# Two layers in one launch on one Trainium2 core: the second layer re-staged into three overlapping stages, and one preparation step of the first layer moved by one unit

## The reference, cut to what matters

```python
# layer 0, xn = layernorm(x)
x = x + L0_attn(xn) + L0_ffn(xn)   # softmax attention with 4x8 heads of 8 and a memory read; NVFP4 MLP, 2048 wide
# layer 1, xn = layernorm(x)
q, k = l2norm_by_head(xn @ Wq.T), l2norm_by_head(xn @ Wk.T)
v    = head_norm(xn @ Wv.T)
xc   = silu(causal_conv(xn))                    # 4 taps
gamma, ig, og = sigmoid(xc @ W.T + b)           # three such products
mem  = scan(mem * gamma + ig * k * v)           # along the sequence
o    = head_norm(head_norm(mem) * q) * gn_g + gn_b
x    = x + (o * og) @ Wo.T + (sigmoid(xn @ w1.T) * (xn @ w2.T)) @ w3.T   # w1, w2, w3 ternary, 704 wide
```

## Time and profile before

| | before |
|---|---|
| median of 3 runs (lowest, highest) | 904.14 us (903.02, 904.34) |
| the profiled execution: its time, its span | 904.06 us, 902.3 us |
| PE, DVE, ACT, POOL busy in the span | 752.3, 647.4, 451.5, 411.1 us |
| mean granted TensorE clock, share of full speed | 0.939 |
| layer 0, up to its last instruction | 609.2 us |
| the four intervals between layer 1's scans, and the last scan to the end | 62.23, 61.84, 60.19, 36.65 us |

### The profile page before, as it was taken

One profiled execution on the slowest core, in us unless ns is written; L12 is line 12 of the kernel. 1 busy time (PEld: TensorE's weight loads), 2 busy tenths in 40 slices (PEclk: granted clock), 3 DMA queues, 4 the chain that ended last, 5 costly groups with the idle time before them and its releaser, 6 DMA issues. The chain is left out here.

```text
span 902.3 us, 15623 instructions
## 1 busy us (share of the span) xinstructions
PE 752.3 (83%) x5602; PEld 645.9 (72%) x5602; DVE 647.4 (72%) x1146; ACT 451.5 (50%) x717; POOL 411.1 (46%) x335
## 2 busy tenths in 40 slices
PE   3268889999999999999999999990888588595843
PEld 3257678888888888888888888880667376484642
DVE  6998976787777767767777776634548949859765
ACT  4256545655655655655655655553534325335300
POOL 2244542343366585485254254334171743824721
PEclk9999998999999999999999999995889889699785
DMA  5011210210001101101000000004000000000000
GB/s 156 22 42 45 85 36 25 55 37 20 19 21 43 43 20 49 42 20 27 19 3 20 20 3 19 3 1 153 1 1 1 1 24 0 0 23 0 0 23 24
DMA packets 21383, 25.82 MB, mean 29 GB/s; under 512 B 4418, under 2 KB 17090, under 8 KB 21060
## 3 DMA queue, kind: packets, MB, share of 16 engines
q1 hardware_dynamic: 21316, 24.93, 9.4%
HBM read 14.83 MB, written 3.28 MB: 20 GB/s over the span
## 5 line engine op out<-in xcount | busy, mean ns | idle before, releaser
L593 DVE TENSOR_REDUCE neg_max<-s_pair 128x4 f32<-128x1024 f32 x127 | 155.0, 1220 | 80.9 <-PE s_pair L805 80.7
L446 ACT ACTIVATE probs<-t_pair 128x1024 f32<-128x1024 f32 x128 | 131.2, 1025 | 139.5 <-PE t_pair L830 139.1
L345 POOL TENSOR_TENSOR hid<-g,hid 128x512 f32<-128x512 f32 x64 | 82.2, 1284 | 185.5 <-DVE g L704 144.2
L339 POOL TENSOR_TENSOR hid_lo<-hid,hid_hi 128x512 fp32r<-128x512 f32 x64 | 85.8, 1340 | 96.6 <-ACT hid_hi L456 96.5
L805 PE MATMUL s_pair<-K,Q 96*128 96x256 f32 x508 | 85.1, 291 | 15.1 <-DVE neg_max L593 9.7
L805 PEld LDWEIGHTS s_pair<-K,Q 96*128 96x128 f32 x508 | 76.0, 195 | 23.8 <-issue 8.1
L830 PE MATMUL t_pair<-Q,K 104*128 104x512 f32 x256 | 85.6, 416 | 0.3 <-DMA Q<-max_parts 0.3
L872 PE MATMUL down<-w_hi,hid_hi 128*128 128x256 f32 x256 | 83.9, 328 | 0.7 <-POOL hid_lo L339 0.7
L872 PE MATMUL down<-w_lo,hid_hi 128*128 128x256 f32 x256 | 72.1, 282 | 0.0
L872 PE MATMUL down<-w_hi,hid_lo 128*128 128x256 f32 x256 | 72.1, 282 | 0.0
L845 PE MATMUL misc<-probs,V 128*32 128x256 f32 x1024 | 69.6, 390 | 2.0 <-DVE a_mem L570 1.0
(11 more groups left out here) (249 smaller groups left out, 1984.4 us busy)
## 6 DMA issues: line engine op xcount, KB each, us to landing
stage<-in_ternary SPq DMA_DIRECT2D x18, 256.0 KB, 2.8
Q<-q_hi SPq DMA_DIRECT2D x64, 64.0 KB, 2.0
stage<-in_scales SPq DMA_DIRECT2D x8, 384.0 KB, 3.4
X<-in_x SPq DMA_DIRECT2D x8, 256.0 KB, 3.8
Q<-q_lo SPq DMA_DIRECT2D x32, 64.0 KB, 2.0
Q<-max_parts SPq DMA_DIRECT2D x128, 4.0 KB
out<-res SPq DMA_DIRECT2D x8, 256.0 KB, 2.2
shared<-in_l1w SPq DMA_DIRECT2D x1, 1536.0 KB, 6.1
```

Of the source, the lines that this page charges most:

```text
L339: pool.tensor_tensor(hid_lo[:, m % 2, :, :].rearrange("p a n -> p (a n)"), hid[:, m % 2, :], hid_hi[:, m % 2, :, :].rearrange("p a n -> p ...
L345: pool.tensor_tensor(hid[:, m % 2, :], g[:, m % 2, :], hid[:, m % 2, :], ALU.mult).then_inc(S["hid_done"], 1)
L446: act.activation(probs[:, u % 2, th, :], t_pair[:], ACT.Exp, scale=SCALE).then_inc(S["probs_done"], 1)
L593: dve.tensor_reduce(neg_max[:, u % 2, 4 * jp:4 * jp + 4], score_banks(u, jp)[:].rearrange("p (s n) -> p s n", n=SEQ), AX_X, ALU.max, negat ...
```

## The change

Layer 1 becomes three stages over turns written out one by one, without the loop: a turn works on a late, an early and an *ahead* group. `normalise`, `xn_turn` (now into banks 6 and 7), `xn_high`, both `xn_low` and the first two taps of the convolution of the next group are done near the end of the turn before. `ffn_down` and `mlp_added` of a group move from its early turn into its late turn: PE has them after `ffn_up(3)`, in banks 4 and 5, and DVE adds them after `output_centered(1)`. The hidden chunks go round in a ring of nine places. `b_turn` of a half waits for the residual of that half. Some ACT steps change places, the new `xn` lies in the memory of `osq`, and the sums of the two late norms are taken out in front (`memory_summed`, `output_summed`). In layer 0 the reciprocals and `mem` products of batch 1 come one unit earlier (`mem` in units 7 and 8), and `SUM_AT` goes from 9 to 10.

```diff
-SUM_AT, GAMMA_AT, SIGN_AT = 9, 21, 22
+SUM_AT, GAMMA_AT, SIGN_AT = 10, 21, 22
...
-                        (5, "mask0"), (5 + late, "recip0"), (6 + late, "recip1"), (8, "qload1"), (8, "mask1")):
+                        (5, "mask0"), (5, "recip0"), (6, "recip1"), (8, "qload1"), (8, "mask1")):
...
-            put(HEADS * (b - 1) + 7 + late + t, "mem", 2 * b + t)
+            put(HEADS * (b - 1) + 7 + t, "mem", 2 * b + t)
...
+            for late, early, ahead in ((None, 0, 1), *((g, g + 1, g + 2) for g in range(GROUPS - 2)), (GROUPS - 2, GROUPS - 1, None), (GROUPS - 1, None, None)):
+                turn(late, early, ahead)
... POOL, end of the turn
                     hidden_low(pool, early, 4)
+                    through_input_gate(pool, early, 0)
+                if ahead is not None:
+                    xn_low(pool, ahead, 1)
+                if early is not None:
                     hidden_low(pool, early, 5)
-                    through_input_gate(pool, early, 0)
                     through_input_gate(pool, early, 1)
... ACT, end of the turn
                     hidden(5)
+                    decays(1)
                     gate(0)
                     gate(1)
...
                     output_high(1)
-                    decays(1)
+                if ahead is not None:
+                    xn_high(ahead, 0)
+                    xn_high(ahead, 1)
                     gate(2)
                     gate(3)
... DVE
-                    normalise()
...
                     scan(0)
                     scan(1)
-                    xn_low(dve, early, 0)
-                    convolve()
+                    convolve(early, range(2, TAPS))
+                    memory_summed()
                     hidden(0)
...
                     output_centered(1)
-                    output_normed()
+                    mlp_added(0)
+                    mlp_added(1)
+                    output_summed()
                     hidden(4)
+                    output_normed()
+                    normalise(ahead)
                     gated(dve, late, 1)
                     hidden(5)
                     output_low(0)
                     output_low(1)
+                    xn_low(dve, ahead, 0)
+                    convolve(ahead, range(0, 2))
                     residual(0)
                     residual(1)
-                    mlp_added(0)
-                    mlp_added(1)
... PE
                 def xn_turn(g, b):
-                    wait("decay_done", 0)
+                    wait("hid_done", 0)
...
                     ffn_up(3)
+                    ffn_down(0)
+                    ffn_down(1)
                     gamma(0)
                     ffn_up(4)
                     gate(0)
                     gate(1)
                     ffn_up(5)
                     gamma(1)
+                    xn_turn(ahead, 0)
+                    xn_turn(ahead, 1)
                     o_turn(0)
                     o_turn(1)
                     gate(2)
                     gate(3)
                     output(0)
                     output(1)
-                    ffn_down(0)
-                    ffn_down(1)
```

More of the change, by code:

```diff
@@ L1132, in waiter, with turns @@
             return wait
[L1134 to L1142, removed]
+        def turns(turn):
+            for late, early, ahead in ((None, 0, 1), *((g, g + 1, g + 2) for g in range(GROUPS - 2)), (GROUPS - 2, GROUPS - 1, None), (GROUPS - 1, None, None)):
+                turn(late, early, ahead)
         def linked(engine, wait, name, steps):
@@ L1154, in linked, with xn_low @@
             return ins
-        def xn_low(engine, early, b):
-            wait = waiter(engine, early)
+        def xn_low(engine, g, b):
+            wait = waiter(engine, g)
             wait("xpad_done", b + 1)
@@ L1217, in _, with turn @@
             pool.memset(xpad[:, :, :, 0:PAD], 0.0).then_inc(pad_zeroed, 1)
-            def turn(late, early):
+            def turn(late, early, ahead):
                 def convolved():
@@ L1251, in _, with turn, xn_high @@
             act.wait_ge(pad_zeroed, 1)
-            def turn(late, early):
-                def xn_high(b):
-                    wait = waiter(act, early)
+            def turn(late, early, ahead):
+                def xn_high(g, b):
+                    wait = waiter(act, g)
                     wait("xn_turned", b + 1)
@@ L1375, in turn @@
                     hidden_high(3)
+                if late is not None:
+                    output_squared(1)
+                if early is not None:
                     sigmoid(4)
@@ L1386, in turn @@
                     output_high(1)
+                if ahead is not None:
+                    xn_high(ahead, 0)
+                    xn_high(ahead, 1)
                 if early is not None:
-                    decays(1)
                     gate(2)
                     gate(3)
-            turns(act, turn)
+            turns(turn)
         @block.vector
         def _(dve):
-            def turn(late, early):
+            def turn(late, early, ahead):
                 links = [0, 0]
@@ L1538, in residual @@
                     wait(f"stored{b}", 0)
-                    at = late * TPG + 2 * b
-                    x = X[:, slice(at, at + 2) if isinstance(late, int) else bass.ds(at, 2), :]
+                    x = X[:, late * TPG + 2 * b:late * TPG + 2 * b + 2, :]
                     inc(dve.tensor_tensor(res[:, b, :, :], turned(banks[4 + b][:]), x, ALU.add), "res_done")
-                if early is not None:
-                    normalise()
+                if late is None:
+                    normalise(early)
+                    xn_low(dve, early, 0)
+                    convolve(early, range(0, 2))
                 if late is not None:
@@ L1579, in turn @@
                     output_low(1)
+                if ahead is not None:
+                    xn_low(dve, ahead, 0)
+                    convolve(ahead, range(0, 2))
+                if late is not None:
                     residual(0)
                     residual(1)
-                if early is not None:
-                    mlp_added(0)
-                    mlp_added(1)
-            turns(dve, turn)
+            turns(turn)
         @block.tensor
@@ L1649, in ffn_down @@
                 def ffn_down(b):
-                    wait = waiter(pe, early)
+                    wait = waiter(pe, late)
                     if b == 0:
@@ L1715, in output @@
                     inc(mm, "y_done")
+                if late is None:
+                    xn_turn(early, 0)
+                    xn_turn(early, 1)
                 if late is not None:
@@ L1751, in turn @@
                     output(1)
-                if early is not None:
-                    ffn_down(0)
-                    ffn_down(1)
-            turns(pe, turn)
+            turns(turn)
 def build(nc, dram, out):
```

123 lines of the change are left out of this document (64 added, 59 removed).

## The result

The changed kernel takes **893.72 us** (median of 4 runs, 892.51 to 894.9), the kernel before 904.24 (4 runs on the same chip, 903.02 to 904.46): ratio **0.9886, interval 0.9867 to 0.9906**. It is faster by 10.5 us. Predicted were 891.0, with 880 to 899 as the range. The profiled execution took 894.9 us, its span 893.1, at a granted clock of 0.942.

What follows compares the result with a forecast made beforehand. Layer 1 was taken as a chain of DVE, then PE, with no engine full; in layer 0 PE was nearly full. Terms -4.2 - 1.8 - 2.6 - 2.5 - 6.9 + 5.0 = -13.0 from 904.14 gave 891 us, range 880 to 899.

Steps and rivals of the forecast that it cites:

- `normalise(ahead)`: Middle turns, between `output_normed` and `gated(1)`: 1.3 us alone, plus 3.0 waiting for POOL (1.2 to 4.3).
- layer 0: Unit 9 loses its `mem` step, -6.9 us; unit 7 +0.7, unit 5 +2.0; in all -4.2 (-5.1 to -2.9).
- fourth turn: Layer 1's turn with nothing ahead: next scan at 53.3 us against 60.19, so -6.9.
- tail: After the last scan `ffn_down` has no cover, so `output_summed` begins later: +5.0 us, up to +7.5.
- The two middle turns: Second and third turn of layer 1, from scan to scan: -2.6 and -2.5 us, the third at 59.3.
- The rival that layer 0 gives nothing: Layer 0: unit 5's reciprocal delays decoding and masks, unit 9's stall only moves; 895 us, chance 0.08.
- `ffn_down` in PE's idle time: Middle turns: its 5.67 us fit PE's 6.39 idle ahead of `gamma(0)`, free with 0.7 to spare, `gamma(0)` at full clock.
- The end of `output_normed`: DVE's front part of a middle turn: ends 39.6 us after the first scan, against 41.88 before.
- The taps: End of a middle turn, two L1438 and two L1441 on DVE: 3.2 us alone, waits for POOL 1.1 to 2.1 more.
- No queue at the memory path: Layer 1's middle turns: `normalise` and the taps cost only what they cost alone; 882 us, chance 0.22.
- Everything paid: Layer 1: every DVE wait for POOL is paid and PE is slow through the gates; 898 to 902 us, chance 0.16.
- The clock, 906 us: Layer 1, turns two to four: PE stays at 1.2 GHz, middle turns' granted clock 0.81 not 0.89; chance 0.09.

Runs made afterwards that it cites:

- the edit alone: The kernel before with only the layer 0 edits of the change: 899.92 us, ratio 0.996.
- the version with early normalisation: The changed kernel with `normalise(ahead)` moved from behind `output_normed` to ahead of it: 884.61 us, ratio 0.9792.
- the kernel with one tap ahead: The changed kernel with only the first tap of the next group's convolution ahead, in place of two: 889.2 us, ratio 0.9835.
- the experiment with banks 6 and 7: The changed kernel with the last group's `ffn_down` in banks 6 and 7, not waiting for `memory_scaled`: 888.58 us, ratio 0.9828.
- without the third stage: The changed kernel with the next group's preparation and all taps back at the start of its own turn, `ffn_down` still late: 885.25 us, ratio 0.9798.
- the three: The changed kernel with normalisation ahead of `output_normed`, last `ffn_down` in banks 6 and 7, and two, one or no tap ahead: 881.24, 878.64, 880.47 us.

## Why the prediction was near, and where it was off

The mechanisms of the prediction held, and DVE's waits for POOL were the right thing to fear. What it had wrong is a size: `normalise(ahead)`, put at 3.0 us over its own time, took 3.9.

Predicted and measured, by its own terms (us; layer 0 from unit 0 to unit 63, the first turn from there to the first scan, the rest from first scan to first scan):

| term | predicted | measured |
|---|---|---|
| layer 0 | -4.2 | 560.95 to 556.75: -4.2 |
| first turn | -1.8 | 87.90 to 86.41: -1.5 |
| second turn | -2.6 | 62.24 to 60.65: -1.6 |
| third turn | -2.5 | 61.84 to 61.65: -0.2 |
| fourth turn | -6.9 | 60.19 to 53.97: -6.2 |
| tail | +5.0 | 36.65 to 39.89: +3.2 |
| sum | -13.0 | -10.5 |

Part of the nearness is luck. The two middle turns together were to fall by 5.1 us and fell by 1.8; the four turns of layer 1 gave 4.3 us less than forecast in all, and the tail, which cost 1.8 less than forecast, gave part of that back.

The span fell by 9.2 us only, because unit 0 began at 33.78 in this execution and at 32.54 in the one before.

**Layer 0: right, by its mechanism and its sum.** Unit 5 went to 13.17 (+1.9, +2.0 predicted), unit 7 to 8.38 (+0.7), unit 9 to 8.30 (-7.0, -6.9 predicted). Beside these three stand two that nobody forecast and that cancel: unit 6, 1.5 us longer in this execution, and unit 31, 11.69 before and 10.16 after. Both have two lengths, as shown above, so it is luck that the sum of -4.2 came out to the tenth; that the three forecast terms did is not. The rival that layer 0 gives nothing is out: the edit alone gave 3.8 us.

**`ffn_down` in PE's idle time: right.** 0.83 us of idle time was left, 0.7 had been predicted, and `gamma(0)` started at full clock.

**The end of `output_normed`: forecast 0.9 us too early.** It ended 778.08 - 737.59 = 40.5 us after the scan, predicted 39.6. `hidden(0)` started 7.85 after the scan and not at about 6.7, for PE came out of an idle time of 2.7 us ahead of `b_turn` at the 1.2 GHz level and had `query_key(0)` (1.05 us for a pair in place of 0.63) and `center_rows` ahead of `ffn_up(0)`; its granted clock was 0.5 from 738.25 to 741.66. DVE idled 1.18 us for the sigmoid. In the second turn the same start was at 6.86; the version with early normalisation has it at 6.27 in two turns. The prediction reckoned with the 1.2 GHz level elsewhere but put no price on it at this place.

**`normalise(ahead)`: the term that was mis-sized.** "I take 3.0, more than one wait and fewer than all": it was 5.31 - 1.38 = 3.9 us, near the upper bound of 4.3. All four operations waited. The reason given for fewer, that a product of POOL's that waits for its own predecessor comes too late to get in, was wrong: POOL's products followed each other with less than 0.1 us between them, and each got in between two of DVE's operations. In the first turn, where POOL had two products there, `normalise` took 3.42, two waits. The experiment with the early normalisation settles it, 1.37 us beside an idle POOL.

The prediction was also unsure whether this form waits at all. It called the strided `normalise` slower by element than a plain operation, let the trace overrule that, and still gave 0.22 to the case in which it goes free. The rows say otherwise: beside an idle POOL the starts of two `L1436` of 512 elements lie 0.45 us apart (788.50 to 789.39 for two) and those of `normalise` of 256 elements 0.32 (765.33 to 766.62 for four), while a product with two tensor inputs, `L1439`, takes 0.68 (4.06 for six) at 512, and one of 64 elements in the inverse root 0.26. Taken as one kind each, a further element costs 0.13 us / 256 = 0.5 ns in the first and 0.42 us / 448 = 0.9 ns in a product (estimates from these four rows). So `normalise` and the first tap run faster by element than the product does. The Trainium skill, "SBUF — State Buffer" (Who interferes with whom), names `tensor_scalar` among the operations that can enter a two-port mode and then contend with GpSimd, and exempts an operation with at most one SBUF input outside such a mode. So its exception was applied to the wrong operation; it fits `gated(1)`, and the traces agree: 5.31 against 1.37 us for `normalise`, 1.43 and 1.43 for the products that read PSUM. Pace alone does not mark who waits, though: `L1439`, the slower product, reads two tensors from SBUF, and its first one beside POOL took 1.76 us in place of 0.74.

**The taps: 0.5 us more than the most likely value.** The two `L1436` took 2.94 and the two `L1439` 2.43 us, 5.2 from the start of the first to the next operation; predicted were 3.2, with one wait in it, plus 1.1 to 2.1. Three of the four operations waited, one for each of POOL's products, and the last did not (0.74 us); beside an idle POOL the four take 0.89 + 1.35 = 2.2. The chain behind: `hidden(5)` ended at 48.4 after the scan (46.5 predicted), `o_turn` at 52.1 (50.4), the last copy at 54.9 (53.0), the taps at 60.2 (57.8), the next scan came at 61.65 (59.3). Of the 2.35 us, 0.9 come from the front, 0.9 from `normalise`, 0.5 from the taps. PE's granted clock was full again from 789.45, at the end of `o_turn`, and PE was not the bound: its outputs ended 795.8, DVE's taps 797.8.

**The fourth turn and the tail: right in kind.** The tail was +3.2 and not +5.0: `ffn_down` started 11.4 us after the scan (11.2 predicted) and took 7.4 (7.4 to 8.7), so that `output_summed` began at 19.45 in place of 14.9, 4.55 late; but the last outputs then ran more at full clock (the 1.2 GHz level lasted 5.7 us from the start of `o_turn`, and 7.5 in the kernel before), and 1.3 us came back. Why is open: PE had been idle 10.73 and not 21.55 us ahead of them, but with the same 10.73 the kernel with one tap ahead had 7.3 us of that level there. The prediction had no term for it. The cause of the delay is shown by the experiment with banks 6 and 7.

**The rivals.** No queue at the memory path: fell, one operation of DVE's waits at each product of POOL's. Everything paid: half came true (all waits paid, PE not slow through the gates). The clock, 906 us: the granted clock of the middle turns stayed at 0.89, far from the 0.81 that it needed.

**Missed by the prediction**: that the third stage as a whole is a loss. The fall of the middle turns by 2.5 us was taken as the sum of its parts, but none of the rivals split it: without the third stage the third turn takes 57.81, and the third stage takes it back to 61.65.

## What to carry to other kernels

A piece moved into "idle" time must be weighed against what the other engines do in that stretch, above all DVE against POOL: the same four operations cost 1.4 or 5.3 us, depending on a place some 6 us earlier or later. When a change has several parts that need each other, price the version without each part too; here all but the third stage won 18.5 us and the third stage gave some 8 of them back, and the sum looked like a success. And take up to the end of a chain only what fits before its other leg ends: one tap was the best of the three, two were too many.

## What the runs showed of the hardware

For DVE's `TENSOR_SCALAR` operations from SBUF to SBUF, DVE and POOL took turns one operation at a time whenever both had one ready: four operations of DVE's of 0.3 us each became 5.31 us beside four of POOL's products (2.99, 1.26 and 1.31 us for 2, 1 and 1), 3.42 beside two, 1.37 beside none. So the price here went by products of POOL's, some 1.3 us each. It was the same for the longer operation: two of 512 elements became 2.94 us beside two products, against 0.98. The products with two inputs from SBUF (`L1439`) waited as well, 1.76 us against 0.74 for one, and those with one input in PSUM did not. By this count four short operations would pay more than one long one; that was not tried. POOL's own products beside `normalise` took no longer: the pair at the start of `gated(0)` 2.99 us there and 3.00 beside the products that read PSUM. Beside the taps they did, a little: 1.48 and 1.46 us for two that take 1.26 and 1.27 elsewhere in the same turn.

After an idle time of some 2 us PE came back at either level: in unit 6 of layer 0, behind the same wait of 1.9 us, a pair of 256-column matmuls took 0.63 us in one execution and 0.40 in another, and the unit 11.3 or 9.8 us. A single profile of this kernel is uncertain by such steps of 1.5 us here and there, so differences of 2 us between kernels rest on the medians, and those within a turn on the rows.
